# Four gated residual layers on one core: the low-rank rows of a pair's two blocks mixed in one step

## What is computed

```
L0: x @ W0.T + 0.5 * (x @ A0[label0[b]]) @ B0.T             rank 32, one of 5 tables per batch
L1: x @ w_eff.T      w_eff from W1 quantised to a codebook, plus a rank-64 delta
L2: x @ W2.T + 0.5 * (x @ A2[label2[b]]) @ B2.T             rank 32, one of 5 tables per batch
L3: x @ W3.T + 2 * sum over experts e of gate[b, t, e] * (x @ A3[e].T) @ B3[e].T
    gate: logits x @ Wr.T, plus 5 at the batch's language id; the best two of 8 experts, softmax
```

## Time and profile before

| | us |
|---|---|
| median of 3 runs (611.38 to 611.91) | 611.8 |
| the profiled execution's own time | 611.85 |
| its span, first to last instruction | 609.9 |
| PE busy | 599.9 |
| PE's weight loads busy (beside PE) | 536.0 |
| DVE busy | 392.5 |
| ACT busy | 214.0 |
| POOL busy | 80.4 |

### The profile page before, as it was taken

How to read it: one execution, slowest core, us unless ns; L and a number is a source line. 1 busy time by engine, 2 the same in 40 slices (tenths; PEclk the granted TensorE clock), 3 DMA queues, 4 the chain that set the end, 5 groups by cost and what they waited for, 6 DMA issues and landing times.

```text
span 609.9 us, 9220 instructions
## 1 busy us (share of the span) xinstructions
PE 599.9 (98%) x3247; PEld 536.0 (88%) x3247; DVE 392.5 (64%) x726; ACT 214.0 (35%) x402; POOL 80.4 (13%) x111
## 2 busy tenths in 40 slices
PE   7999999999999999999999999899999999999998
PEld 7999999899999999888888687688888888888887
DVE  3589998999998829100005688957474747475653
ACT  4444133346233138211111378433333333333331
POOL 2101010023000000000000015040404040403120
PEclk9999999999999999999999999999999999999999
DMA  9963220361000030200001200121221213130201
GB/s 266 261 170 99 82 70 1 43 218 68 1 1 1 1 35 7 38 1 0 0 0 34 69 2 2 52 87 54 85 75 63 82 56 98 39 118 19 96 8 70
DMA packets 57823, 37.68 MB, mean 62 GB/s; under 512 B 26684, under 2 KB 51516, under 8 KB 57796
## 3 DMA queue, kind: packets, MB, share of 16 engines
q1 hardware_dynamic: 57796, 37.31, 21.8%
HBM read 28.91 MB, written 8.39 MB: 61 GB/s over the span
## 4 chain that ended last, share of the span: by engine, by line
PE 85%; DVE 10%; ACT 2%; DMA 2%; issue 1%; SPq 0%; POOL 0%; DVEq 0%
PE acc L1356 46%; PE acc L1493 27%; PE acc L1514 4%; DVE q L1010 2%; PE acc L1516 2%; PE aux L1343 2%; DVE hg_lo L1036 1%; PE acc L1522 1%; DVE qtmp L1009 1%; PE acc L1523 1%; PE aux L1431 1%; DMA a_t<-in_L_cond_Wr_dram 1%; PE acc L1343 1%; DVE w_lo L914 1%; DMA w_raw<-in_L_cond_lora_B_w_dram 1%
## 5 line engine op out<-in xcount | busy, mean ns | idle before, releaser
L1356 PE MATMUL acc<-hg_hi,w_hi 128*128 128x352 f32 (+2 forms) x384 | 87.2, 335 | 0.4 <-DVE hg_lo L921 0.4
L1356 PE MATMUL acc<-hg_lo,w_hi 128*128 128x352 f32 (+2 forms) x384 | 85.8, 331 | 0.0
L1356 PE MATMUL acc<-hg_hi,w_lo 128*128 128x352 f32 (+2 forms) x384 | 85.7, 331 | 0.0
L1356 PEld LDWEIGHTS acc<-hg_hi,w_hi 128*128 128x128 f32 x384 | 66.3, 188 | 1.7 <-DVE hg_lo L921 0.6
L1356 PEld LDWEIGHTS acc<-hg_hi,w_lo 128*128 128x128 f32 x384 | 67.3, 188 | 0.0
L1356 PEld LDWEIGHTS acc<-hg_lo,w_hi 128*128 128x128 f32 x384 | 67.3, 188 | 0.0
L914 DVE TENSOR_TENSOR w_lo<-a_t,w_hi 128x1024 fp32r<-128x1024 f32 (+2 forms) x9 | 9.9, 1106 | 82.1 <-ACT w_hi L596 82.1
L1010 DVE TENSOR_TENSOR q<-q,qtmp 128x1024 f32<-128x1024 f32 x48 | 60.0, 1250 | 1.7
L761 ACT CAST left_hi<-xr 128x512 fp32r<-128x512 f32 x64 | 39.7, 622 | 54.4 <-PE acc L1493 34.7
L1493 PE MATMUL acc<-rh_a,left_hi 128*128 128x512 f32 (+1 forms) x132 | 52.7, 399 | 0.0
L532 POOL TENSOR_TENSOR xr<-xr 128x512 f32<-128x512 f32 x28 | 35.5, 1287 | 130.5 <-DVE left_lo L1159 129.2
(11 more groups left out here) (213 smaller groups left out, 1041.8 us busy)
## 6 DMA issues: line engine op xcount, KB each, us to landing
x_st<-in_x_dram SPq DMA_DIRECT2D x64, 128.0 KB, 2.8
out_dram<-part SPq DMA_DIRECT2D x31, 256.0 KB, 2.8
g<-in_L_cond_W_dram SPq DMA_DIRECT2D x8, 512.0 KB, 7.3
w_st<-in_L_cond_W_dram SPq DMA_DIRECT2D x8, 512.0 KB, 4.7
a_t<-in_L_cond_weight_dram SPq DMA_DIRECT2D x8, 512.0 KB, 5.0
w_raw<-in_L_cond_weight_dram SPq DMA_DIRECT2D x8, 512.0 KB, 4.0
a_raw<-in_L_cond_lora_A_dram SPq DMA_DIRECT2D x5, 128.0 KB, 3.6
a_raw<-in_L_cond_lora_A_dram SPq DMA_DIRECT2D x20, 32.0 KB, 2.0
```

Source lines behind the costliest of these rows:

```text
L1356: last = pe.matmul(acc[0:a.shape[-1], slot, bank * BANK:bank * BANK + c1 - c0], a[:, k, :], b[:, k, c0:c1], start=(at == 0 and n == 0), st ...
```

## The change

The two blocks' low-rank rows are kept side by side (`vt` and `vm` now hold both blocks) and mixed by two matmuls of 256 columns, in product W, where `mix(1)` stood; `mix(0)` in product Y is gone. ACT and DVE turn the result into `vm` with one `m_high` and one `m_low`. `correct_others(0)` goes from ahead of product W to behind it, next to `correct_others(1)`. `turn_g(0)` goes from product X (S2), after three of its slices, to product Z (S1), after two; `turn_g(1)` goes from after one slice of X (S3) to after two. On DVE `best_two(0)` and `gated(0)` go behind left S1 and the one `m_low`; `g_low(0)` keeps its place behind `gated(1)`. POOL's mixer waits for the pair's one count of `mix_done` instead of its two. The places of `vt` in SBUF and of the mixed and gated rows in `aux` change with that.

```diff
--- before.py
+++ after.py
@@ -214,10 +214,10 @@
         b3_hi = place("b3_hi", 32768, [P, D], F32R)
         vb_hi, vb_lo = place("vb_hi", 79616, [P, C_LOW2], F32R), place("vb_lo", 205824, [P, C_LOW2], F32R)
         tsel_h, tsel_l = place("tsel_h", 36864, [P, P], F32R), place("tsel_l", 37376, [P, P], F32R)
-        vm = [place(f"vm{h}", 37888 + 512 * h, [P, P], F32R) for h in range(2)]
+        vm = place("vm", 37888, [P, 2, P], F32R)
         hgt_h = [place(f"hgt_h{h}", 38912 + 512 * h, [P, P], F32R) for h in range(2)]
         hgt_l = [place(f"hgt_l{h}", 39936 + 512 * h, [P, P], F32R) for h in range(2)]
-        v_sb, vt = place("v_sb", 40960, [P, 2, 2 * R]), place("vt", 41472, [P, P], F32R)
+        v_sb, vt = place("v_sb", 40960, [P, 2, 2 * R]), place("vt", 203776, [P, 2, P], F32R)
         hg = place("hg", 126720, [P, E, RE])
         gate = place("gate", 127232, [P, 96])
         top_i = place("top_i", 127616, [P, 8], U32)
@@ -241,6 +241,10 @@
 
         def aux_at(h, n):
             return aux[:, h * BANK + n * P:h * BANK + (n + 1) * P]
+
+
+        AUX_MIX = aux[:, P:3 * P]
+        AUX_GATED = (aux[:, BANK + 2 * P:BANK + 3 * P], aux[:, 3 * P:4 * P])
 
         w3_in = [sem(f"w3_in{k}") for k in range(KT)]
         small_in, tables_in, a3_in, a2_in = sem("small_in"), sem("tables_in"), sem("a3_in"), sem("a2_in")
@@ -582,7 +586,7 @@
                 l0, l2 = label(0, b), label(1, b)
                 pool.wait_ge(e_split, b + (E_FIRST - 1))
                 select_both(l0, l2)
-                pool.wait_ge(mix_done, b * 2)
+                pool.wait_ge(mix_done, b)
                 mixer(l2)
                 pool.wait_ge(tsel_ready, b * 2 + 2)
                 left_sums(b)
@@ -842,15 +846,15 @@
 
                 def v_high(h):
                     act.wait_ge(v_tr, b * 2 + (h + 1))
-                    act.copy(vt[:], aux_at(h, 0)).then_inc(v_hd, 1)
-
-                def m_high(h):
-                    act.wait_ge(mix_done, b * 2 + (h + 1))
-                    act.copy(vm[h][:], aux_at(h, 1)).then_inc(m_hd, 1)
+                    act.copy(vt[:, h], aux_at(h, 0)).then_inc(v_hd, 1)
+
+                def m_high():
+                    act.wait_ge(mix_done, b + 1)
+                    act.copy(vm[:].rearrange("p h r -> p (h r)"), AUX_MIX).then_inc(m_hd, 1)
 
                 def g_high(h):
                     act.wait_ge(g_tr, b * 2 + (h + 1))
-                    act.copy(hgt_h[h][:], aux_at(h, 2)).then_inc(g_hd, 1)
+                    act.copy(hgt_h[h][:], AUX_GATED[h]).then_inc(g_hd, 1)
 
                 def exponential(h):
                     act.wait_ge(d_ready, b * 2 + (h + 1))
@@ -867,14 +871,13 @@
                     right_high("T2", 3)
                 copy_second(1)
                 left_high(b, "S2")
-                m_high(0)
                 v_high(1)
                 if first:
                     copy_part("M1", "X")
                     right_high("T1", 3)
                 done("M2")
                 left_high(b, "S1")
-                m_high(1)
+                m_high()
                 exponential(0)
                 if first:
                     act.copy(b3_hi[:], b3_f[:]).then_inc(b3_hd, 1)
@@ -1224,17 +1227,17 @@
 
                 def v_low(h):
                     dve.wait_ge(v_hd, b * 2 + (h + 1))
-                    dve.tensor_tensor(vt[2 * R:], aux_at(h, 0)[2 * R:], vt[2 * R:].bitcast(F32),
+                    dve.tensor_tensor(vt[2 * R:, h], aux_at(h, 0)[2 * R:], vt[2 * R:, h].bitcast(F32),
                                       ALU.subtract).then_inc(v_split, 1)
 
-                def m_low(h):
-                    dve.wait_ge(m_hd, b * 2 + (h + 1))
-                    dve.tensor_tensor(vm[h][2 * R:], aux_at(h, 1)[2 * R:], vm[h][2 * R:].bitcast(F32),
-                                      ALU.subtract).then_inc(m_split, 1)
+                def m_low():
+                    dve.wait_ge(m_hd, b + 1)
+                    low = vm[2 * R:].rearrange("p h r -> p (h r)")
+                    dve.tensor_tensor(low, AUX_MIX[2 * R:], low.bitcast(F32), ALU.subtract).then_inc(m_split, 1)
 
                 def g_low(h):
                     dve.wait_ge(g_hd, b * 2 + (h + 1))
-                    dve.tensor_tensor(hgt_l[h][:], aux_at(h, 2), hgt_h[h][:].bitcast(F32),
+                    dve.tensor_tensor(hgt_l[h][:], AUX_GATED[h], hgt_h[h][:].bitcast(F32),
                                       ALU.subtract).then_inc(g_split, 1)
 
                 lg, top, idx, g0, g1 = (gate[:, 8 * n:8 * n + 8] for n in (0, 1, 2, 4, 5))
@@ -1280,16 +1283,14 @@
                     right_low("T4", 3)
                 v_copy(1)
                 left_low(b, "S2")
-                m_low(0)
                 v_low(1)
                 if first:
                     right_low("T2", 3)
-                best_two(0)
-                m_low(1)
-                gated(0)
-                if first:
                     right_low("T1", 3)
                 left_low(b, "S1")
+                m_low()
+                best_two(0)
+                gated(0)
                 best_two(1)
                 left_low(b, "S4")
                 gated(1)
@@ -1519,8 +1520,8 @@
 
                 def finish(bank, h, half, c=slice(0, HD)):
                     cols, at = slice(half * HD + c.start, half * HD + c.stop), BANKS[bank][:, c]
-                    pe.matmul(at, vm[h][:], vb_hi[:, cols], start=False, stop=False, skip_group_check=True)
-                    pe.matmul(at, vm[h][:], vb_lo[:, cols], start=False, stop=False, skip_group_check=True)
+                    pe.matmul(at, vm[:, h], vb_hi[:, cols], start=False, stop=False, skip_group_check=True)
+                    pe.matmul(at, vm[:, h], vb_lo[:, cols], start=False, stop=False, skip_group_check=True)
                     three(at, (hgt_h[h][:], hgt_l[h][:]), (b3_hi[:, cols], b3_lo[:, cols]),
                           stop=True).then_inc(step_done, 1)
 
@@ -1528,27 +1529,29 @@
                     pe.wait_ge(v_out, b * 2 + (h + 1))
                     turn_tile(aux_at(h, 0), v_sb[:].rearrange("p u c -> p (u c)")).then_inc(v_tr, 1)
 
-                def mix(h):
-                    pe.wait_ge(v_split, b * 2 + (h + 1))
+                def mix():
+
+                    pe.wait_ge(v_split, b * 2 + 2)
                     pe.wait_ge(tsel_ready, b * 2 + 2)
-                    pe.matmul(aux_at(h, 1), tsel_h[:], vt[:], start=True, stop=False, skip_group_check=True)
-                    pe.matmul(aux_at(h, 1), tsel_l[:], vt[:], start=False, stop=True,
+                    rows = vt[:].rearrange("p h r -> p (h r)")
+                    pe.matmul(AUX_MIX, tsel_h[:], rows, start=True, stop=False, skip_group_check=True)
+                    pe.matmul(AUX_MIX, tsel_l[:], rows, start=False, stop=True,
                               skip_group_check=True).then_inc(mix_done, 1)
 
                 def correct_others(h):
-                    pe.wait_ge(m_split, b * 2 + (h + 1))
+                    pe.wait_ge(m_split, b + 1)
                     if first:
                         pe.wait_ge(vb_hd, 4)
                         pe.wait_ge(vb_done, 5)
                         pe.wait_ge(vb_zero, 1)
                     at = E_BANK[h][:, EH:E_W]
-                    pe.matmul(at, vm[h][:], vb_hi[:, D:C_LOW2], start=False, stop=False, skip_group_check=True)
-                    pe.matmul(at, vm[h][:], vb_lo[:, D:C_LOW2], start=False, stop=True,
+                    pe.matmul(at, vm[:, h], vb_hi[:, D:C_LOW2], start=False, stop=False, skip_group_check=True)
+                    pe.matmul(at, vm[:, h], vb_lo[:, D:C_LOW2], start=False, stop=True,
                               skip_group_check=True).then_inc(r_done, 1)
 
                 def turn_g(h):
                     pe.wait_ge(hg_ready, b * 2 + (h + 1))
-                    turn_tile(aux_at(h, 2), hg[:].rearrange("p e r -> p (e r)")).then_inc(g_tr, 1)
+                    turn_tile(AUX_GATED[h], hg[:].rearrange("p e r -> p (e r)")).then_inc(g_tr, 1)
 
                 def wait_left(name):
                     pe.wait_ge(l_split, count(b, LEFT, name))
@@ -1580,30 +1583,28 @@
                 others(1, range(5, KT)).then_inc(step_done, 1)
 
                 wait_out("C11")
-                product("Y", "A12", "B21", range(1), start=True)
-                mix(0)
-                product("Y", "A12", "B21", range(1, 2))
+                product("Y", "A12", "B21", range(2), start=True)
                 turn_v(1)
                 product("Y", "A12", "B21", range(2, HALF)).then_inc(step_done, 1)
-                correct_others(0)
 
                 if first:
                     pe.wait_ge(acc_free, 2 + PASSES)
                 wait_out("C21")
                 product("W", "A22", "T4", range(1), start=True)
-                mix(1)
+                mix()
                 product("W", "A22", "T4", range(1, HALF)).then_inc(step_done, 1)
+                correct_others(0)
                 correct_others(1)
 
                 wait_left("S2")
```

(12 more changed lines are left out.)

## The result

The changed kernel took **624.85 us** (median of 4 runs, 624.54 to 625.22) against 611.86 us before: a ratio of 1.021, with an interval of 1.020 to 1.023. Forecast was 623.7 us, slower. The profiled execution took 624.54 us, its span is 622.4 us, 12.5 us over the 609.9 of before.

A forecast was written before the change was run, and what follows sets the result against it. PE was taken to bound the kernel, with DVE a third of a microsecond under it. First pair +1.6, second +1.3, six more +8.9: +11.8 us on 611.85 gives 623.7 us, own range 622.2 to 625.2.

The forecast's parts named there:

- Need 7.65 us against cover 6.03: Time from second `correct_others(0)` matmul to block 0's finish: 7.65 us needed through DVE, 6.03 us of PE work covering it.
- the stall: PE idle ahead of `finish("Y", 0, 0)` in every pair, forecast at 1.6 us.
- The sum: Added time over the eight pairs: first +1.6, second +1.3, six more at +1.49 giving +8.9; together +11.8 us.
- the second pair: Second pair's added time: +1.5 us less the 0.2 it waited before at block 0's finish, so +1.3.
- the two margins: Slack behind the stall: 0.4 us for `g_low(1)`, 0.2 to 0.3 us for C22 before the next pair; both taken as costing nothing.
- The unknown prices: Copies over 256 columns: `m_high` on ACT 0.27 us to twice that, `m_low` on DVE 0.29 to 0.58; upper ends taken.
- The correction's wait for them: `correct_others(0)` waiting for the mixed rows' copies behind W: nothing, or about 0.1 us with S1 in the way; taken as nothing.
- The merged mix: One mix of two 256-column matmuls on PE, 0.24 us instead of 0.46: 0.22 us less per pair, 1.8 us in eight.
- Rival 2: A second wait, at `g_low(1)` or C22, late by 0.4 us in seven pairs: +2.8, 626.5 us; chance 9%.
- Rival 1: DVE's gating stays hidden within PE's 6.03 us and PE's gain remains: 610.1 us, 5%; 1% for near 611.8.
- Rival 3: TensorE's clock falls to 1.2 GHz behind each stall: +22 us, 646; chance 3%.
- the forecast's signs: Expected in the profile after: 1.4 to 1.6 us idle before each finish, 16 fewer matmuls, PE busy under 600 us, clock 1.00.

The follow-up runs named there:

- experiment 1: Kernel before, with the changed kernel's order on PE and DVE but still two mixes of 128 columns: 625.93 us.
- experiment 3: Changed kernel with `g_low(0)` moved on DVE ahead of `gated(1)`, in the first pair the split of B3 with it: 621.66 us.
- experiment 4: Changed kernel with the wide mix at the end of product Y and both corrections ahead of W's last slice: 619.00 us.
- experiment 6: Changed kernel with `g_low(0)`, transposes, `g_low(1)` early on DVE, mix ending Y, corrections after two slices of W, mixed rows' copies ahead of S1's: 610.65 us.
- experiment 2: Two runs on the changed kernel: left S4 behind `g_low(0)` on DVE, 623.01 us; block 0's finish behind two slices of X (S3), 622.30 us.

## Why the prediction was right, step by step

- **The mechanism held.** Need 7.65 us against cover 6.03, with `g_low(0)` queued behind `gated(1)`: the stall was forecast at 1.6 us, and the profile has 1.45 us of idle (a matmul's row reaches 0.16 past its neighbour's start, which the idle leaves out). Experiments 1, 3 and 4 show each half of it: the move makes the stall, `gated(1)` in front of the split keeps it, an earlier start shortens it by as much.
- **The sum.** The finish of block 0 against before: first pair +1.85 us (388.08), forecast +1.6; second +1.71, forecast +1.3; the next six together +8.87 (421.50 to 609.14 against 417.94 to 596.71), forecast +8.9. With 0.07 behind the last that is the 12.5 us; forecast 11.8. The rest of the 1.15 us between 623.7 and 624.85 lies outside the sum: 2.1 us around the span instead of 1.95, and a median 0.3 above the profiled execution.
- **What was off: the second pair, by 0.4.** I took off 0.2 us because the kernel before "waited before" there. That idle was the weight load's alone; from combine to finish that pair took 8.66 us like all others, so it had lost nothing. The other 0.2: its gating ran 0.12 longer than the next pairs' (7.44 against 7.31 us), and its first product waited for C22, one of the two margins that the forecast had called small and left at nothing. In the first pair DVE started at 379.42 (forecast 379.27) and took 0.15 longer.
- **The unknown prices** fell inside their bounds: ACT's copy of 256 columns 0.37 us (0.27 to 0.54), DVE's 0.43 (0.29 to 0.58). The correction's wait for them cost nothing, as forecast: DVE was done at 444.2 and then idle for 1.28 us.
- **The merged mix.** Two matmuls of 256 columns 0.11 us apart, worth 0.21 us a pair (experiments 1 and 6), 0.22 forecast from the narrow ones' 0.23 us. The prediction says that the stall swallows this gain, but its sum has the 0.22 in it, and the sum is right: the gain is there in stalled pairs too (31.31 against 31.52 us). The Trainium skill's N / 2.4 GHz + 2.5 ns ("TensorE: Matmul & The Clock Gate", section "Wait — 56ns, not 53.3ns?") fits the wide pair (0.109 us) and not the narrow pair, each of whose matmuls loads weights of its own; no run here tells whether that is why.
- **Rival 2** (a second wait behind the first) did not decide in the steady pairs, but it was 0.3 us away. Taking my stall for the only limit made the expectations of experiments 2 and 3 wrong by 3 to 10 us. **Rival 1** could not be: DVE needed 7.3 us. **Rival 3**, the clock, is below; with it went two of the forecast's signs, a clock of 1.00 and PE busy for under 600 us (601.8).

## What to carry to other kernels

When a dependent step is moved later in one engine's queue, price the run of work on the other engine between it and its deadline against what is left of the first engine's work: here 7.65 against 6.03 us, and the difference came eight times. A stall is a reading of the tightest limit only, so before counting on its removal, look for the next one (here a buffer freed by the same engine, a load and a sum, 0.3 us behind). And a saving on the busiest engine, 0.2 us a pair, counts under the stall as well where it lies between the finish and DVE's next start, but it made the kernel faster than before only after the waits were gone.

## What was not expected of the hardware

**The clock in the first pair.** PE's timeline behind the 2.8 us stall, and the windows around it (length, busy times of PE, PEld, DVE, ACT, POOL, then the granted clock):

```profile
388.42 0.39 PE L1524 MATMUL acc<-vb_lo,vm 128*128 128x512 f32 x1
...
389.25 0.63 PE L1494 MATMUL acc<-b_hi,hgt_l 128*128 128x512 f32 x1
389.68 0.63 PE L1494 MATMUL acc<-rh_a,left_hi 128*128 128x512 f32 x1
```

```profile
385.00:389.00 4.00, 1.20 (x6) 0.79 (x5) 3.79 (x12) 3.02 (x6) 0.00 (x0) 0.99 0.00 0
389.00:393.00 4.00, 4.00 (x13) 3.04 (x12) 4.00 (x8) 0.89 (x2) 0.00 (x0) 0.58 0.00 0
393.00:397.00 4.00, 4.00 (x20) 3.20 (x19) 3.57 (x7) 1.11 (x2) 0.00 (x0) 1.00 0.69 197
```

The granted clock is 0.58 on average from 389 to 393: the lower level, 1.2 GHz, for most of it. Matmuls of 512 columns start 0.43 us apart instead of 0.23, some eight of them. So rival 3 did happen, in one pair and not in eight. The Trainium skill's "TensorE: Matmul & The Clock Gate" (section "What's actually happening") has it that a TensorE that was idle gets the lower clock. The trace agrees for this gap; the seven of 1.3 to 1.6 us kept 1.00. The length of the gap alone does not decide: behind 2.81 us of idle in experiment 1 the mean clock of the execution stayed 1.000, and so it did in experiment 2's first execution, with gaps of 2.31 and 1.79 us; in experiment 3 it fell behind a gap of 1.77 us (0.54 from 394 to 397 us), with gaps of 1.12 and 0.96 us in the 9 us before it. In the changed kernel it cost next to nothing, since what follows waits for DVE in the first pair anyway: from that finish to the finish of block 1 took 5.71 us, 5.59 before, and the changed kernel's run with a mean clock of 1.000 took 624.93 us, in the middle of the others. What makes the clock fall behind one gap and not behind another of the same length is open.

**PE's busy time.** The lower clock is one part of its growth: from 388.89 to 392.64 PE took 3.75 us for what took 2.17 in experiment 1 (388.76 to 390.93, clock 1.00), 1.6 us more. It is not the only one: experiment 1's execution, with a clock of 1.000 throughout, has PE busy for 602.4 us, 2.5 over before. Each stall adds about 0.27 us of busy time, an estimate from the rows: the 0.16 us of the last matmul that nothing hides, and 0.11 until the second one starts; for six stalls more than before that is 1.6 us. Against both stand the 1.8 us of the merged mixes. So a stalled engine can look busier while it does less.
